# Grouped attentions: running maxima turned by VectorE in blocks, two sine tables, and a rearranged row of turns

## What is computed

```python
q = rms_norm(split_heads(q_in @ Wq), q_norm_w)        # 16 heads of 128
k = rms_norm(split_heads(kv_in @ Wk), k_norm_w)       # 4 heads of 128
v = split_heads(kv_in @ Wv)
q, k = rope(q, q_positions), rope(k, all_positions)   # layer 1 alone
scores = einsum("bhqd,bhkd->bhqk", q, repeat(k, 4)) * 128 ** -0.5
out = einsum("bhqk,bhkd->bhqd", softmax(scores), repeat(v, 4)) @ Wo
```

## Time and profile before

| | us |
|---|---|
| median of 3 runs | 3530.37 (3530.24 to 3533.05) |
| the profiled execution | 3520.77 |
| its span, first to last instruction | 3519.0 |
| score tiles of the stage with rope, first to last | 532.8 to 1617.2 |
| score tiles of the stage without rope | 2414.3 to 3364.5 |

### The profile page before, as it was taken

The page is one execution under the profiler, slowest core; times in us unless marked ns, Lnnn a source line. Parts: engine busy times, 40 slices in busy tenths (PEclk is TensorE's granted clock), DMA queues, the critical chain, the costliest instruction groups (busy, mean ns, idle before and its releaser), DMA issues. The chain is left out here.

```text
span 3519.0 us, 63774 instructions
## 1 busy us (share of the span) xinstructions
PE 3264.8 (93%) x23076; PEld 2831.8 (80%) x23076; DVE 2333.8 (66%) x4613; ACT 2247.6 (64%) x5204; POOL 1561.2 (44%) x1568
## 2 busy tenths in 40 slices
PE   6758968999999999998899999897999999999989
PEld 5658957989989989997666665586999999999878
DVE  8976756776676676666777777435666655655554
ACT  3426746777777777775566676415777777777743
POOL 0003127777676667663121120103555555555534
PEclk8879979999999999998999999899999999999999
DMA  5206522211120120102101100213221121111011
GB/s 194 94 17 245 208 106 70 88 62 37 43 80 31 37 92 31 37 25 83 43 1 39 38 1 1 78 39 117 78 81 61 43 74 43 69 60 36 27 40 40
DMA packets 74456, 227.81 MB, mean 65 GB/s; under 512 B 7780, under 2 KB 29472, under 8 KB 69152
## 3 DMA queue, kind: packets, MB, share of 16 engines
q1 hardware_dynamic: 67538, 184.04, 14.7%
q0 software_dynamic: 3696, 37.68, 2.8%
q10 hardware_dynamic: 2910, 2.01, 0.2%
HBM read 178.60 MB, written 45.11 MB: 64 GB/s over the span
## 5 line engine op out<-in xcount | busy, mean ns | idle before, releaser
L1199 PE MATMUL ps<-a_v_rows,a_ring 128*128 128x129 f32 (+1 forms) x7168 | 933.3, 275 | 7.4 <-DVE a_o_rows L1592 6.4
L1564 DVE SCALAR_TENSOR_TENSOR a_peak<-ps,a_k_rstd,a_peak 128x512 f32<-128x512 f32 (+1 forms) x768 | 572.4, 745 | 505.5 <-ACT a_ring L1301 502.3
L1199 PEld LDWEIGHTS ps<-a_v_rows,a_ring 128*128 128x128 f32 (+1 forms) x7168 | 876.6, 191 | 26.3 <-ACT a_ring L1316 6.1
L1301 ACT ACTIVATE a_ring<-ps,a_k_rstd 128x512 f32<-128x512 f32 (+1 forms) x896 | 615.2, 687 | 429.6 <-PE ps L1189 386.1
L1424 POOL TENSOR_TENSOR a_ring<-a_ring,a_negb 128x512 f32<-128x512 f32 (+1 forms) x506 | 649.9, 1306 | 236.9 <-ACT a_negb L1310 229.0
L1316 ACT ACTIVATE a_ring<-a_ring 128x512 f32<-128x512 f32 (+1 forms) x896 | 562.8, 631 | 41.2 <-DVE a_ring L1581 27.7
L1187 PE MATMUL ps<-a_qt,a_kt 128*128 128x512 f32 (+1 forms) x896 | 425.2, 475 | 21.6 <-DVE a_peak L1564 17.4
L1092 PEld LDWEIGHTS ps<-a_wr,a_ct 128*128 128x128 f32 (+1 forms) x2496 | 352.7, 188 | 49.7 <-issue 14.0
L1092 PE MATMUL ps<-a_wr,a_ct 128*128 128x256 f32 (+1 forms) x2496 | 371.2, 286 | 13.9 <-DMA a_ct<-ctx_lo 13.7
L1189 PE MATMUL ps<-a_qt,a_kt 128*128 128x512 f32 (+1 forms) x896 | 355.5, 397 | 0.0
L1188 PE MATMUL ps<-a_qt,a_kt 128*128 128x512 f32 (+1 forms) x896 | 354.4, 396 | 0.0
(11 more groups left out here) (462 smaller groups left out, 6008.4 us busy)
## 6 DMA issues: line engine op xcount, KB each, us to landing
a_wr<-a_w SPq DMA_DIRECT2D x96, 512.0 KB, 4.4
a_w<-a_wr SPq DMA_DIRECT2D x32, 512.0 KB, 3.9
a_wr<-a_w SPq DMA_DIRECT2D x48, 256.0 KB, 3.3
a_ct<-ctx_hi SPq DMA_DIRECT2D x8, 1090.0 KB, 5.5
a_ct<-ctx_lo SPq DMA_DIRECT2D x8, 1090.0 KB, 8.7
f_we<-in_f_experts SPq DMA_DIRECT2D x8, 1088.0 KB, 8.4
ctx_hi<-a_ct SPq DMA_DIRECT2D x4, 1602.0 KB, 5.4
ctx_lo<-a_ct SPq DMA_DIRECT2D x4, 1602.0 KB, 9.3
```

The lines of the kernel that those rows point to most:

```text
L1199: ins = pe.matmul(m.ps[:, 6 + i // 2, (i % 2) * 256:(i % 2) * 256 + VW], slot(n)[0:r, i * P:(i + 1) * P], v_rows[u // NG % 2][0:r, t, :], ...
L1301: act.activation(slot(n)[0:r, :], m.ps[0:r, SCORE_BANKS[n % 2], :], ACT.Copy, scale=k_rstd[0:r, g % 2, t:t + 1]).then_inc(kept, 1)
L1564: dve.scalar_tensor_tensor(out=peak[0:r, :], in0=m.ps[0:r, SCORE_BANKS[n % 2], :], scalar=k_rstd[0:r, u // NG % 2, t:t + 1], in1=(slot(n - ...
```

## The change

- The running maxima are turned by VectorE: right behind a unit's last `highest`, `turn_maxima` transposes `peak` in 32x32 blocks into the unit's half of `negb` (which its shifts on POOL have left by then), the turn's shift follows, and `fold_maxima` reduces each block's rows to one value, `folds` (128 x 16). MX on TensorE is one transpose of `folds` to 16 x 128, behind a wait for `folded`. MX on VectorE takes the lowest of the negated values over four parts, writes the 16 x 32 result into PSUM, and multiplies it with a 0/1 pattern (`eights`) into `spread`, 16 x 256. NB is two matmuls of 256 columns over 16 rows (`halves` picks eight of the sixteen).
- The angles are made in the sine table of the batch to come, of which there are now two, and the sines are taken in place. Waits of RS and RA0 for the old table's last reader go or become far older ones.
- In the stage with rope the row of turns is rearranged: Y0 goes from turn 0 to 4, Y1 from 4 to 5, KX3 from 5 to 7, QN, QR, KR0 and KR1 a turn earlier, most gathers later.
- In the stage without rope the VectorE shifts of a unit are tiles 2, 6, 10 instead of 3, 7, 11; its row of turns stays.

```diff
@@ -715,11 +715,11 @@
 True: (
-    "Y0< KR6< PR0 GP4 GP5 GP6 GP7", "MX1 KR7<", "NB1 KX2< W0< PX0", "Q0 RA0 GA12< GA13<", "Y1< RS0 GA14< GA15<", "KX3<",
-    "Q1", "W2<", "KV0 QN0 GA4 GA5", "KV1 QN1 GA6 GA7", "KV2 QR0", "KV3 QR1 RA1 RA2", "OX0 KN0 QR2", "KV4 QR3", "KV5 KR0",
-    "KV6 W1 KR1 RA3 GP8", "MX0 GP9", "NB0 QX0 GP10", "KV7 RA4 GP11", "KX0 KN1", "KV8 KR2", "KV9 KR3", "KV10 RA5 RA6 GA8",
-    "OX1 N0 GA9", "KV11 GA10", "KX1 KN2 GA11", "KV12 KR4 RA7 GP12", "KV13 KR5 NZ0 GP13", "KV14 RA8 GP14",
-    "QX1 KN3 NX0 GP15",
+    "KR6< PR0 GP4 GP5 GP6 GP7", "MX1 KR7<", "NB1 KX2< W0< PX0", "Q0 RA0", "Y0< RS0", "Y1<", "Q1", "KX3< W2< QN0",
+    "KV0 QN1 GA8<", "KV1 QR0 GA9<", "KV2 QR1 GA10<", "KV3 QR2 RA1 RA2 GA11<", "OX0 KN0 QR3", "KV4 KR0", "KV5 KR1 GP12<",
+    "KV6 W1 RA3 GP13<", "MX0 GP14<", "NB0 QX0 GP15<", "KV7 RA4", "KX0 KN1", "KV8 KR2", "KV9 KR3", "KV10 RA5 RA6 GA4 GA12<",
+    "OX1 N0 GA5 GA13<", "KV11 GA6 GA14<", "KX1 KN2 GA7 GA15<", "KV12 KR4 RA7 GP8", "KV13 KR5 NZ0 GP9", "KV14 RA8 GP10",
+    "QX1 KN3 NX0 GP11",
 ),
@@ -830,20 +830,21 @@
 peak = st.sb("peak", [P, 512])
-negmax = st.sb("negmax", [P, 2, JG], F32R)
+folds = st.sb("folds", [P, 16])
+halves = st.sb("halves", [16, 2], F32R)
+eights = st.sb("eights", [16, 8])
+spread = st.sb("spread", [16, 256], F32R)
 negb = st.sb("negb", [P, 2, 512])
 ring = st.sb("ring", [P, RING, 512])
 rsum = st.sb("rsum", [P, JG])
 o_rows = st.sb("o_rows", [P, NJ, HD])
 ot = [st.sb(f"ot{i}", [P, NJ * P], F32R) for i in range(2)]
 if rope:
-    cs = st.sb("cs", [P, 2, KT, half])
+    cs = [st.sb(f"cs{i}", [P, 2, KT, half]) for i in range(2)]
     pos_i = st.sb("pos_i", [KT, P], I32)
     pos_rows = st.sb("pos_rows", [KT, P])
     pos_f = st.sb("pos_f", [P, KT])
     invf = st.sb("invf", [P, half])
-    ang_tmp = st.sb("ang_tmp", [P, 2, KT, half])
-    ang, tmp = ang_tmp[:, 0, :, :], ang_tmp[:, 1, :, :]
     by_cos = st.sb("by_cos", [P, 4 * HD])
@@ -859,7 +860,7 @@
      "st_ready kept peaked shifted exp_done pv_done o_done").split()]
-shifted_dve = st.sem("shifted_dve")
+shifted_dve, squared_up, folded = [st.sem(n) for n in "shifted_dve squared_up folded".split()]
 o_turned, o_hi, o_lo = [st.sem(n) for n in "o_turned o_hi o_lo".split()]
@@ -873,7 +874,7 @@
     return t % 3 > 0
-return t % 4 > 0 and t < KT - 2 if rope else t % 4 == 3
+return t % 4 > 0 and t < KT - 2 if rope else t % 4 == 2
 
@@ -900,6 +901,15 @@
 
+def tables_of(g):
+
+    return cs[((g + 1) // KVH if attend else 0) % 2]
+
+def angles_of(g):
+
+    tables = cs[(g // KVH + 1 if attend else 0) % 2]
+    return tables[:, 1, :, :], tables[:, 0, :, :]
+
 def tokens_of(g):
@@ -916,6 +926,8 @@
     return z[:, j % 2, :]
+if attend:
+    return flat2(cs[1][:, j % 2, 0:4, :])
 return flat2(o_rows[:, 2 * (j % 2):2 * (j % 2) + 2, :])
@@ -1150,10 +1162,8 @@
 out = begin(("MX", g, i))
-pe.wait_ge(peaked, peaks(KT * (unit_of(g, i) + 1) - 1))
-for j in range(JG):
-    ins = pe.transpose(out[:, j * P:(j + 1) * P], peak[:, j * P:(j + 1) * P], m.ident[:, :])
-ins.then_inc(item_ready, 1)
+pe.wait_ge(folded, unit_of(g, i) + 1)
+pe.transpose(out[0:16, 0:P], folds[:, :], m.ident[:, :]).then_inc(item_ready, 1)
 
@@ -1162,10 +1172,9 @@
     pe.wait_ge(shifted_dve, shifts[True][KT * u - 1])
-for j in range(JG):
-    ins = pe.matmul(m.ps[:, MAX_BANK, j * P:(j + 1) * P],
-                    negmax[:, u % 2, j:j + 1].to_broadcast([P, P]), m.ident_r[:, :],
-                    start=True, stop=True)
+for h in range(2):
+    ins = pe.matmul(m.ps[:, MAX_BANK, h * 256:(h + 1) * 256],
+                    halves[:, h:h + 1].to_broadcast([16, P]), spread[:, :], start=True, stop=True)
 ins.then_inc(spread_ok, 1)
@@ -1305,8 +1314,6 @@
 act.wait_ge(spread_ok, u + 1)
-if u >= 2:
-    act.wait_ge(shifted, shifts[False][KT * (u - 1) - 1])
 act.activation(negb[:, u % 2, :], m.ps[:, MAX_BANK, :], ACT.Copy).then_inc(negb_ok, 1)
@@ -1316,11 +1323,9 @@
 def RS(g, _i):
-    if attend:
-        act.wait_ge(k_ready, rotated_k[("KR", g - 1, 2 * len(KB) - 1)])
-    for i, (angle, table) in enumerate(((ang, cs[:, 1, :, :]), (tmp, cs[:, 0, :, :]))):
-        act.wait_ge(angles, 2 * (turn_of_batch(g) - 1) + i + 1)
-        act.activation(table, angle, ACT.Sin).then_inc(tab_ok, 1)
+    act.wait_ge(angles, 2 * turn_of_batch(g))
+    for angle in angles_of(g):
+        act.activation(angle, angle, ACT.Sin).then_inc(tab_ok, 1)
 
@@ -1399,8 +1404,8 @@
 pool.wait_ge(item_free, number[("KV", g, t1 - 1)] + 1)
-products(rows, n, cs[:, 0, t0:t1, :].unsqueeze(2).to_broadcast([P, n, 2, half]),
-         cs[:, 1, t0:t1, :].unsqueeze(2).to_broadcast([P, n, 2, half]))
+products(rows, n, tables_of(g)[:, 0, t0:t1, :].unsqueeze(2).to_broadcast([P, n, 2, half]),
+         tables_of(g)[:, 1, t0:t1, :].unsqueeze(2).to_broadcast([P, n, 2, half]))
 
...
@@ -1559,17 +1564,35 @@
         dve.wait_ge(peaked, peaks(n - 1))
-    elif u:
-        dve.wait_ge(item_ready, number[("MX", u // NG, 1 - u % NG)] + 1)
     dve.scalar_tensor_tensor(out=peak[0:r, :], in0=m.ps[0:r, SCORE_BANKS[n % 2], :],
                              scalar=k_rstd[0:r, u // NG % 2, t:t + 1],
                              in1=(slot(n - 1) if t == 1 else peak)[0:r, :],
                              op0=ALU.mult, op1=ALU.max).then_inc(peaked, 1)
 
+def turn_maxima(u):
+
+    blocks = negb[:, u % 2, :]
+    if u >= 2:
+        dve.wait_ge(shifted, shifts[False][KT * (u - 1) - 1])
+    dve.wait_ge(peaked, peaks(KT * (u + 1) - 1))
+    dve.transpose(blocks, peak[:, :]).then_inc(squared_up, 1)
+
+def fold_maxima(u):
+
+    dve.wait_ge(squared_up, u + 1)
+    dve.tensor_reduce(folds[:, :].unsqueeze(2),
+                      negb[:, u % 2, :].rearrange("p (b k) -> p b k", k=32),
+                      AX.X, ALU.max).then_inc(folded, 1)
+
 def MX(g, i):
 
-    src = begin(("MX", g, i)).rearrange("p (j n) -> p j n", j=JG)
-    dve.tensor_reduce(negmax[:, unit_of(g, i) % 2, :].unsqueeze(2), src, AX.X, ALU.max, negate=True)\
+    out = begin(("MX", g, i))
+    lowest = out[0:16, P:P + 32]
+    src = out[0:16, 0:P].rearrange("b (k q) -> b q k", q=32)
+    step(dve.tensor_reduce(lowest.unsqueeze(2), src, AX.X, ALU.max, negate=True))
+    dve.tensor_tensor(spread[:, :].rearrange("b (c q) -> b c q", c=8),
+                      eights[:, :].unsqueeze(2).to_broadcast([16, 8, 32]),
+                      lowest.unsqueeze(1).to_broadcast([16, 8, 32]), ALU.mult)\
        .then_inc(item_free, 1)
@@ -1618,11 +1641,12 @@
 PI = 3.1415925
+ang, tmp = angles_of(g)
 if i == 0:
     if not attend:
         dve.wait_ge(freq_in, 16)
-    if turn_of_batch(g) > 1:
-        dve.wait_ge(tab_ok, 2 * (turn_of_batch(g) - 1))
+    if attend and g > KVH:
+        dve.wait_ge(k_ready, rotated_k[("KR", g // KVH * KVH - 2, 2 * len(KB) - 1)])
     step(dve.tensor_tensor(ang, pos_f[:, :].unsqueeze(2).to_broadcast([P, KT, half]),
@@ -1648,6 +1672,9 @@
     dve.wait_ge(zeroed, ZEROED)
+    for h in range(2):
+        step(dve.tensor_reduce(halves[:, h:h + 1], m.ident[0:16, 8 * h:8 * h + 8], AX.X, ALU.max))
+    step(dve.tensor_tensor(eights[:, :], m.ident[0:16, 0:8], m.ident[0:16, 8:16], ALU.add))
 does = {"GA": GA, "PR": PR, "PX": PX, "RA": RA, "W": W, "N": N, "NZ": NZ, "NX": NX, "KV": KV, "Q": Q,
@@ -1660,8 +1687,12 @@
     highest(n)
+if attend and n < TURNS and n % KT == KT - 1:
+    turn_maxima(n // KT)
 if attend and 0 <= s < TURNS and by_turn[s]:
     shift(s)
+if attend and n < TURNS and n % KT == KT - 1:
+    fold_maxima(n // KT)
 for task, g, i in turn:
```

More of the change, by code:

```diff
@@ L1413, in QR @@
                         pool.wait_ge(q_scaled, normed_q[("QN", g, q)])
-                        products(rows, REP, cs[:, 0, CTILES + q, :].unsqueeze(1).unsqueeze(1).to_broadcast([P, REP, 2, half]),
-                                 cs[:, 1, CTILES + q, :].unsqueeze(1).unsqueeze(1).to_broadcast([P, REP, 2, half]))
+                        products(rows, REP, tables_of(g)[:, 0, CTILES + q, :].unsqueeze(1).unsqueeze(1).to_broadcast([P, REP, 2, half]),
+                                 tables_of(g)[:, 1, CTILES + q, :].unsqueeze(1).unsqueeze(1).to_broadcast([P, REP, 2, half]))
                     def shift(n):
@@ L1525, in KR @@
                         dve.wait_ge(item_free, number[("KV", g, t1 - 1)] + 1)
-                        dve.tensor_tensor(bs, rows, cs[:, 1, t0:t1, :].unsqueeze(2).to_broadcast([P, n, 2, half]), ALU.mult)
-                        step(dve.tensor_tensor(bc, rows, cs[:, 0, t0:t1, :].unsqueeze(2).to_broadcast([P, n, 2, half]),
+                        dve.tensor_tensor(bs, rows, tables_of(g)[:, 1, t0:t1, :].unsqueeze(2).to_broadcast([P, n, 2, half]), ALU.mult)
+                        step(dve.tensor_tensor(bc, rows, tables_of(g)[:, 0, t0:t1, :].unsqueeze(2).to_broadcast([P, n, 2, half]),
                                                ALU.mult))
```

## The result

The changed kernel takes 3516.4 us in the median of 6 runs (3511.9 to 3521.4), the kernel before 3531.1 us (6 runs, 3528.3 to 3533.1). The ratio is 0.9958 with a 95% interval of 0.9945 to 0.9971: 14.6 us less, where the forecast had 37 less and a range that ended at 3513. The direction was right; the size was not.

A forecast was written before the change was run, and what follows sets the result against it. TensorE's busy time was taken to bound both stages. The terms 30.6 - 1.2 - 6.6 + 4.2 + 4.5 + 8.5 - 3 = 37 us, off a median of 3530.4, gave 3493 us, range 3475 to 3513.

The forecast's parts named there:

- NB, four 128- to two 256-column matmuls: At each unit's end on TensorE: NB would cost 0.24 us, saving 0.15 with rope and 0.21 without.
- fold late in turn 1, rope: Ordinary rope groups: TensorE's MX would wait up to 0.1 us for the fold, -1.2 us over 12 groups.
- RA8 and the waits of groups 3, 7, 11: Rope groups after a batch is prepared: RA8 delays the last maximum, TensorE loses 2.2 us each, -6.6 in all.
- sines, turn 7: Rope stage: moved Y1 and KX3 would cover turn 7's two waits after the sines, 1.4 x 3 = +4.2 us.
- gathers, groups 0 and 1: Rope stage: moving gathers later removes 7 us of waits, less 2.5 for their new place, net +4.5 us.
- vector shift ahead of NB: Stage without rope: shifting tile 10 instead of 11 ends NB's 0.53 us wait, 16 x 0.53 = +8.5 us.
- tails: Last unit of both stages: Y0 is owed and transpose and fold stand in the chain, -3 us.
- the TensorE term: Shorter MX and NB over all units save 32.6 us, less 2 for first and last groups: 30.6 us.
- rival 4: NB waits for MX's product each group and gathers cost as before: 24 us less, 3506, chance 0.11.
- rival 5: POOL lengthens VectorE's block transpose and fold, so each unit's MX waits: slower, 3549, chance 0.05.
- Rival 3: Matmul time follows columns, so NB saves nothing: 26 us less in all, 3504, chance 0.10.
- cases 1 to 4: The rivals on the fast side: 3493 (0.56), 3481 (0.14), 3504 (0.10), 3506 (0.11); faster was given 0.92.

The follow-up runs named there:

- e8: Changed kernel with NB over 128 zero-filled rows, the angles' VectorE steps spread (RA8 in turn 24) and the fold right behind the block transpose: 3482.1 us, ratio 0.9866.
- e7: Kernel before with one edit: without rope, VectorE shifts tiles t % 4 == 2 instead of t % 4 == 3; 3518.9 us, ratio 0.9972.
- e1: Changed kernel with the operands of NB's two matmuls zero-filled from 16 to 128 rows: 3500.7 us, ratio 0.9908.
- e3: Kernel before with the maxima part alone (block transpose, fold, 16-column MX, 16-row NB, moved shift tiles), old row of turns: 3521.1 us, ratio 0.9972.
- e5: Like e1, but NB's matmuls read 64 rows of the zero-filled operands: 3519.2 us in one run.
- e6: Like e1, but NB's matmuls read 32 rows of the zero-filled operands: 3516.1 us in one run.
- e2: Changed kernel with the angles' VectorE steps at other turns in the rope stage, RA8 from turn 28 to 24: 3506.8 us, ratio 0.9930.
- e4: Kernel before with the two sine tables and the new row of turns alone, maxima the old way: 3522.1 us, ratio 0.9976.

## Why the prediction was wrong, step by step

| term | forecast | measured | from |
|---|---|---|---|
| MX, four transposes to one | 64 x 0.33 = 21 | 0.33 a unit | timeline after, |
| NB, four 128- to two 256-column matmuls | +11.5 (0.15 and 0.21 a unit) | -9 or so (tiles 0.14 to 0.15 longer) | tile lengths |
| fold late in turn 1, rope | -1.2 | about -2 (0.18 x 12) | e8 |
| RA8 and the waits of groups 3, 7, 11 | -6.6 | -6.7 (2.23 x 3) | timeline after |
| clock behind those waits | not in the sum | -5.8 in the profiled run | groups 76.9, 74.1, 72.6 |
| sines, turn 7 | +4.2 | 1.4 x 3 | after: 0.59 left of 2.02 |
| gathers, groups 0 and 1 | +4.5 | +4.7 | groups of 55.9 and 68.5, before 60.0 and 69.1 (61.6 and 69.1 in e7, with the same code) |
| vector shift ahead of NB | +8.5 | +8.9 between medians, +11.7 by the stage | e7 |
| first groups without rope | not in the sum | -3: groups 1 to 4 in all 2.3 longer than groups of their kind later on, group 0 0.8 longer than before | group lengths after |
| tails | -3 | 1.9 and 1.4 us of wait for the fold, of which 0.6 stood before at NB | TensorE's waits |

**The step that failed is the price of NB**: "Twelve such matmuls take 1150.79 to 1152.20, 0.118 us each, so NB costs 0.24". Those twelve (Y) have 128 rows; NB's have 16. A tile with NB grew from 2.45 to 2.60 us with rope and from 2.08 to 2.22 without, where it should have shrunk by 0.15 and 0.21; e1 brings both to 2.28 and 1.83. That is 0.33 us x 64 = 21 us on paper and 15.7 between the medians; in e1's profile the clock cost groups 3, 7 and 11 no less than in the changed kernel's (73.4, 74.6, 73.5 us), and groups 0, 1, 2, 6, 10 and 14 with rope gained only 0.1 to 0.3 us instead of 0.66. The lower bound of that term ("if a 256-column matmul cost two 128-column ones, NB would save nothing") was no bound: it let the columns vary and never the rows. By measure the TensorE term is 64 x (0.33 - 0.15) = 12 instead of 30.6, and e3 and e7 have the same ratio to the kernel before, 0.9972: of the maxima part's gain the shift tile alone is all that can be measured. What MX saved, NB, the waits at groups 3, 7 and 11 and those of the first groups without rope gave back.

This also ends near the estimated 11 us that the prediction had put beside its sum from the Trainium skill (TensorE: Matmul & The Clock Gate, Back-to-back issue gap), but not for that reason: each transpose removed was worth 0.11 us, not 56 ns, and two 256-column matmuls over 128 rows do save against four of 128 columns (2.45 to 2.28 us with rope).

A rule that points at this step stands on another page, without a number, and the prediction did not weigh it. The Trainium skill (TensorEngine Tiling (Array Packing), Key Properties) says that going from one tiling mode to another drains TensorE. In its section Available Configurations the Trainium skill lists tiles of 128, 64 and 32 rows. The runs agree as far as they go: 16, 32 and 64 rows among matmuls of 128 cost the same, 65 and 96 cost nothing extra. Two things in the runs it does not say: the second of two NB matmuls, in the same mode as the first, is also 0.10 us late; and MX's weight of 16 columns among 128 costs nothing (0.23 in, 0.11 out).

**The second step is an omission.** The RA8 paragraph took its loss as the waits alone. Their sizes were right: 2.19 and 1.10 where 0.83 and 0.23 stood, with Y0's 1.41 owed, 2.2 us a group. The granted clock was in none of its ends. Of twelve such starts of a group (the changed kernel, e1, e5 and e6, three groups each) ten had a stretch at the lower level behind the wait of 2.2 us. In groups 7 and 11 of e5 it begins 4.4 and 4.2 us into the group, right behind the first wait (which ends at 4.0) and ahead of the second (0.76 and 0.53 us there), so the second wait can't be its only cause; in e2 and e8, without these two waits, none of six had one, nor had the profile before with 0.83 and 0.22. For the same waits the changed kernel's three groups differ by 4.3 us. That the clock follows the waits is shown by e2 as far as one edit can: it took the waits away and the low stretches went with them. Such stretches have other occasions too (e7, below). What decides between the groups with equal waits was not found.

Put right, the sum is 37 - 18.6 (30.6 to 12) - 5.8 (clock) = 12.6 us, against 14.6 measured, with an interval from 10 to 19. Two smaller misses of the sum nearly cancel: the vector shift by the stage (+3.2) and the first groups without rope (-3).

**What held.** The order of reading did: in a group without idle time on TensorE only the length of its instructions counts, and that is where the miss was found. The steady wait of the earlier trace rows went and gave at least its size; from group 5 on no other wait took its place, while in groups 1 to 4 the one of rival 4 did in part. POOL did not lengthen the block transpose (0.711 to 0.714 us in all 64) or the fold (0.664 to 0.689; rival 5), and the row of turns gave what was added up for it. Rival 3 (3504) named the right instruction with the wrong reason, and was still 12 us short. The forecast of 3493 fits the change with a 128-row NB and without the clock's loss, an estimated 3495: e1's 3500.7 less 5.7, by which its groups 3, 7 and 11 exceed three of 71.9 (the changed kernel's 72.6 without a low stretch, less e1's 0.7). Its chances did not add up: cases 1 to 4 sum to 0.91, not 0.92, and the slower case stands with 0.05 and with 0.04.

## What to carry to other kernels

Before you price a TensorE instruction by a like one, match rows as well as columns: here filling 16 rows up to 128 with zeros, for nothing in the loop, was worth as much again as the change itself. Price a wait of TensorE by the distance between starts and not by its idle time: here 0.53 us of idle time cost 0.77. When waits of TensorE of 1 to 2 us come in an otherwise full stretch, reckon with a loss of granted clock on top (here 0 to 4.3 us each time), and look for the operation on the other engine that makes them. A VectorE operation that takes five times its usual length beside POOL is best moved to a turn where POOL does something small, rather than hidden where it stands.

## What the runs showed of the hardware

- Two fp32r matmuls of 256 columns among 128-row ones cost 0.25 us with 128 rows and some 0.55 with 64, 32 or 16. Their weight loads are not longer: 0.183 us in the median, where the loads of 128 rows in the NB of e7 take 0.190. In the records the load of 64, 32 or 16 rows starts 0.18 us after the start of the matmul before it, in the median, and that of 128 rows (e1) together with it. The Trainium skill (TensorE: Matmul & The Clock Gate, LDWEIGHTS) says that a load's time goes by columns and not by rows; the records agree, and it is no statement about the start of what follows.
- A TENSOR_SCALAR over 128x960 elements took 0.65 us beside a small POOL operation and 3.45 to 3.50 us in 24 of 24 cases (the eight kernels with RA8 in turn 28, three groups each) beside the same sequence of POOL's shift and two products on SBUF, ending some 0.5 us after the third. Another TENSOR_SCALAR of that size (RA2, L1655) took 1.62 to 1.63 us in the changed kernel, ending 0.5 us after a single POOL product. The Trainium skill (SBUF — State Buffer, SBUF: two separate sides) has VectorE's two-port operations and GpSimd exclude each other from one port pair, each for a whole instruction; that such an operation can sit out three POOL instructions, and not only one, is what these rows add.
- The granted clock fell from 1.00 to 0.50 at TensorE's pair of waits (2.2 us, then 0.5 to 1.1 us) in ten cases of twelve, and stayed low for 3 to 10 us; behind 0.8 and 1.6 us (e3) in two of three, behind 2.2 alone (e4) in one of three, and in e7 once in turn 7 behind waits of 1.1 and 0.9 us, where the same waits of the kernel before left it alone.
